# Attention over 7x7 windows: probabilities as the stationary operand, values as 18 moving columns

## The reference

```python
# layer 0: a convolution whose weights are made from the image itself, then a residual
# layer 1: a shifted-window transformer block
h = layer_norm(x); h = roll(h, (-3, -3)); xw = windows_7x7(h).reshape(-1, 49, 48)
q, k, v = split(xw @ w_qkv + b_qkv)             # 6 heads of 8 channels; q scaled
attn = q @ k.T + rel_bias + window_mask         # 49 x 49 for each window and head
attn = softmax(attn)                            # over the keys
o = attn @ v                                    # 49 x 8 for each window and head
x = x + unroll(o @ w_proj + b_proj)
y = layer_norm(x); y = conv3x3(y, 48 -> 192); y = gelu(bn1(y)); y = conv1x1(y, 192 -> 48)
return x + bn2(y)
```

## Time and profile before

| | |
|---|---|
| median of three runs | 4128.19 us |
| span of the profiled execution (the page gives no other time for it) | 4125.0 us |
| layer 0 | 0 to about 494 us |
| attention | about 494 to 2757 us |
| feed-forward | from there to the end |
| TensorE matmul busy, share of the span | 96% |
| weight load, VectorE, ScalarE, GpSimd | 72%, 66%, 59%, 57% |
| DMA | 210.38 MB moved, mean 51 GB/s |

### The profile page before, as it was taken

How to read it: one execution, slowest core, us unless ns; L and a number is a source line. 1 busy time by engine, 2 the same in 40 slices (tenths; PEclk the granted TensorE clock), 3 DMA queues, 4 the chain that set the end, 5 groups by cost and what they waited for, 6 DMA issues and landing times. The chain is left out here.

```text
span 4125.0 us, 76120 instructions
## 1 busy us (share of the span) xinstructions
PE 3958.8 (96%) x23156; PEld 2953.8 (72%) x23156; DVE 2712.5 (66%) x5076; ACT 2451.7 (59%) x4724; POOL 2335.8 (57%) x2216
## 2 busy tenths in 40 slices
PE   7888799999999999999999999969999999999999
PEld 3555577777777777777777777747777777777776
DVE  4454388888888888888888888854444444444443
ACT  3333177777777777777777777744444444444444
POOL 1111266666666666666666666635656565656554
PEclk8888799999999999999999999979999999999999
DMA  4331201111111111111111111125454545454442
GB/s 101 94 94 47 59 20 27 27 26 25 26 27 27 27 27 27 27 26 26 27 27 27 26 25 27 27 52 91 72 95 73 94 74 91 77 87 80 85 83 45
DMA packets 219355, 210.38 MB, mean 51 GB/s; under 512 B 113968, under 2 KB 214320, under 8 KB 216240
## 3 DMA queue, kind: packets, MB, share of 16 engines
q1 hardware_dynamic: 219312, 209.86, 25.1%
HBM read 132.00 MB, written 77.76 MB: 51 GB/s over the span
## 5 line engine op out<-in xcount | busy, mean ns | idle before, releaser
L1222 POOL TENSOR_TENSOR hid_lo<-hid,hid_hi 96x448 fp32r<-96x448 f32 x448 | 770.7, 1725 | 583.2 <-ACT hid_hi L1295 583.1
L590 POOL TENSOR_TENSOR kex<-ks,cw 112x294 f32<-112x294 f32 x1024 | 727.6, 745 | 88.2 <-ACT ks L852 88.2
L1292 ACT ACTIVATE hid<-ps_h,cw 96x448 f32<-96x448 f32 x448 | 323.6, 722 | 728.4 <-PE ps_h L1243 728.4
L683 PEld LDWEIGHTS ps_o<-pt,vex 98*118 98x118 f32 x6144 | 695.1, 183 | 56.4 <-ACT pt L882 2.6
L683 PE MATMUL ps_o<-pt,vex 98*118 98x118 f32 x6144 | 727.0, 268 | 0.5 <-ACT pt L882 0.5
L1354 DVE SCALAR_TENSOR_TENSOR xr<-ps_f,cw,xr 48x448 f32<-48x448 f32 x224 | 151.3, 676 | 773.7 <-PE ps_f L1254 773.7
L656 PE MATMUL ps_s<-kex,qbd 112*98 112x294 f32 x2048 | 592.0, 411 | 0.0
L1239 PE MATMUL ps_h<-ya_hi,wa_hi 128*96 128x448 f32 x1344 | 501.4, 373 | 28.8 <-DVE yb_sp L1328 28.8
L1239 PE MATMUL ps_h<-ya_hi,wa_lo 128*96 128x448 f32 x1344 | 498.6, 371 | 0.0
L1239 PE MATMUL ps_h<-ya_lo,wa_hi 128*96 128x448 f32 x1344 | 498.3, 371 | 0.0
L1015 DVE TENSOR_TENSOR s<-s,mx 98x588 f32<-98x588 f32 x512 | 466.5, 911 | 17.5
(11 more groups left out here) (153 smaller groups left out, 7081.4 us busy)
## 6 DMA issues: line engine op xcount, KB each, us to landing
ya<-y_chunks SPq DMA_DIRECT2D x64, 532.9 KB, 6.9
y_chunks<-y SPq DMA_DIRECT2D x256, 76.1 KB, 1.8
xin<-x_chunks SPq DMA_DIRECT2D x256, 73.5 KB, 2.5
x_chunks<-xo SPq DMA_DIRECT2D x256, 73.5 KB, 1.8
out<-xr SPq DMA_DIRECT2D x32, 588.0 KB, 8.2
yb<-y_chunks SPq DMA_DIRECT2D x96, 177.6 KB, 8.2
xr<-x_chunks SPq DMA_DIRECT2D x32, 514.5 KB, 5.5
xt<-x SPq DMA_DIRECT2D x16, 840.0 KB, 17.2
```

The costliest lines, as they stand in the source:

```text
L590: pool.tensor_tensor(kex[a][:, win, :, :], ks[:, win, :].unsqueeze(1).to_broadcast([PP, HEADS, N]), w("head").unsqueeze(2).to_broadcast([P ...
L683: mm = pe.matmul(ps_o[0:OP, (win % 4) * OP:(win % 4 + 1) * OP], vex[a][:, win, j, 0:OP], pt[d % 2][:, start:start + OP], start=j == 0, sto ...
L1222: pool.tensor_tensor(hid_lo[:, U % slots, :], hid[:, U % slots, :], hid_hi[:, U % slots, :], ALU.subtract).then_inc(hid_lo_set, 1)
L1292: act.activation(hid[:, U % slots, :], ps_h[U % slots][0:half, 0:T1], ACT.Gelu, bias=w("t1")[:, U % 2:U % 2 + 1], scale=w("s1")[:, U % 2:U ...
```

## The change

Transposed probabilities: `pt` gets one buffer for each of the four duos, and holds key rows by (window, head pair, image, query). `values` runs once per half chunk (four windows). For each window, head pair and image there is one matmul: stationary are the 49 columns of `pt` for that image, moving are 18 columns of `vs` (8 channels of the one head, 8 of the other, and two columns of ones, one per head). Image 0 writes PSUM partitions 0 to 48, image 1 writes 64 to 112, so the result has queries on the partitions. VectorE takes the reciprocal of the two sums per query and multiplies (`outputs`), giving `on`. TensorE turns it back to channels on partitions (`outputs` on TensorE: 16 matmuls against the identity `pick`, 49 columns moving, the images again in the two column halves), and ScalarE copies it to `ot` for `project`. `denominators`, the two reciprocal steps on ScalarE and the product on GpSimd are gone.

Further edits: the twelve operations that fill `vex` become two per chunk (product with an ownership mask `own`). The subtraction of the maximum for duo 1 moves from VectorE to GpSimd. The scale and shift of `y` move from VectorE to ScalarE. GpSimd copies the second half of `h` instead of computing it again. The residual is loaded from DRAM by two more DMAs per chunk instead of being made from `xin` on VectorE, and its bias is added within the residual sum. Preparation loses the zeroing of `vex` and 32 small copies.

```diff
 # buffers
-        vex = [sb(f"vex{a}", [2 * N, NWC, HEADS // 2, 2 * BO]) for a in range(2)]
+        vs = [sb(f"vs{a}", [2 * N, NWC * 2 * (HEADS // 2), VW]) for a in range(2)]
-        pt = [sb(f"pt{i}", [2 * N, 2 * HN + OP - 2 * N]) for i in range(2)]
+        pt = [sb(f"pt{d}", [2 * N, 2, HEADS // 2, 2, N]) for d in range(DUOS)]
 # TensorE (QP = 64 + 49, VW = 18)
-            def values(n, d, a):
+            def values(n, half, a):
...
+                for i in range(4):
+                    win = 4 * half + i
                     for j in range(HEADS // 2):
-                        start = i * HN + j * 2 * N
-                        mm = pe.matmul(ps_o[0:OP, (win % 4) * OP:(win % 4 + 1) * OP], vex[a][:, win, j, 0:OP],
-                                       pt[d % 2][:, start:start + OP], start=j == 0, stop=j == HEADS // 2 - 1)
+                        for img in range(2):
+                            block = (win * 2 + img) * (HEADS // 2) + j
+                            mm = pe.matmul(ps_o[BO * img:BO * img + N, (i * (HEADS // 2) + j) * VW:(i * (HEADS // 2) + j + 1) * VW],
+                                           pt[win // 2][:, win % 2, j, img, :], vs[a][:, block, :], start=True, stop=True)
+            def outputs(n, a):
+                pe.wait_ge(o_set, n * 2 + 2)
+                if at_edges(n + 1)[2]:
+                    pe.wait_ge(v_set, n * 2 + 5)
+                for win in range(NWC):
+                    for img in range(2):
+                        mm = pe.matmul(ps_m[1][BO * img:BO * img + C, win * N:(win + 1) * N], on[a][:, win, :],
+                                       w("pick")[:, img * N:(img + 1) * N], start=True, stop=True)
 # TensorE body of chunk n
                 scores(n, 0, a)
-                    values(n - 1, 2, 1 - a)
...
                 scores(n, 1, a)
-                    values(n - 1, 3, 1 - a)
+                    values(n - 1, 1, 1 - a)
...
                 scores(n, 2, a)
                     variance2(n - 2)
-                values(n, 0, a)
                     pe.wait_ge(ln2_done, n - 1)
...
-                    denominators(n - 1, 1 - a)
                 transposes(n, 1)
                 scores(n, 3, a)
-                        pe.wait_ge(lnd_done, n)
                     keys(n + 1)
                     value_rows(n + 1, 0)
-                values(n, 1, a)
+                values(n, 0, a)
+                    outputs(n - 1, 1 - a)
                     value_rows(n + 1, 1)
                 transposes(n, 2)
                     project(n - 1)
 # GpSimd body: split_squares(n+1), split_squares2(n-2), then
-                    normalize2(n - 2, m - 1, a)
-                    twice(n + 1)
-                    divide(n - 1, 1 - a)
+                shift(n)                # tensor_tensor subtract, 98 x 588, duo 1
+                    before_twice(n + 1)
+                    normalize2(n - 2, m - 1, a)
+                    twice()             # tensor_copy(h[:, :, 1, :], h[:, :, 0, :])
                     keys(n + 1, 1 - a)
 # ScalarE: outputs(n - 1, 1), reciprocals(n - 1), outputs(n, 0) gone from the body; new
+                    y_affine(n - 2, a)  # after exps(n, 2)
+                    outputs(n - 1)      # last: ot <- ps_m[1]
 # VectorE
+            def outputs(n, half, a):
+                dve.reciprocal(rden[half][:, :]..., part[:, :, 2 * HD:VW]).then_inc(rden_set, 1)
+                dve.wait_ge(rden_set, n * 2 + half + 1)
+                dve.tensor_tensor(on[a]..., part[:, :, 0:2 * HD]..., rden[half]...to_broadcast(...), ALU.mult).then_inc(o_set, 1)
-                for head in range(HEADS):
-                    ins = dve.tensor_scalar(to[...], rows[:, :, :, own], w("couple")[:, head % 2:head % 2 + 1], None, op0=ALU.mult)
+                dve.tensor_tensor(vs[a][:, half * blocks:(half + 1) * blocks, 0:2 * HD], ps_m[1 - half]..., w("own")..., ALU.mult)
 # SyncE, per chunk: load_ahead(n), load_residual(n), store(n - 2)
+            def load_residual(n, a):
+                if at_edges(n)[0]:
+                    sp.wait_ge(x2_set, n - 1)
+                for i in range(2):
+                    sp.dma_start(xres[a][BO * i:BO * i + C, :, :], x1s[n, C * i:C * i + C, :]...).then_inc(xres_in[a], 16)
```

More of the change, by code:

```diff
@@ L53 @@
 CHUNKS = RC * B // 2
-OP = BO + C + HEADS
+QP = BO + N
+VW = 2 * HD + 2
 HN = HEADS * N
@@ L463, in attention @@
         y_out = [sem(f"y_out{a}") for a in range(2)]
-        wrapped, xres_set = sem("wrapped"), sem("xres_set")
+        xres_in = [sem(f"xres_in{a}") for a in range(2)]
+        wrapped = sem("wrapped")
         center_mm, xc_copied, squared, var_mm, ln_done, rstd_done, h_done, h_twice = (
@@ L536, in _ @@
             load(1, 1)
-            load_ahead(0, 0)
-            load_ahead(1, 1)
+            sp.wait_ge(zeroed, 1)
+            for n in range(2):
+                load_residual(n, n)
+            for n in range(2):
+                load_ahead(n, n)
             with sp.Fori(1, CHUNKS // 2 - 1) as m:
@@ L541, in _ @@
                     load_ahead(m * 2 + a, a)
+                    load_residual(m * 2 + a, a)
                     store(m * 2 + a - 2, a)
-            for n in range(CHUNKS - 4, CHUNKS):
+            for n in range(CHUNKS - 2, CHUNKS):
+                load_residual(n, n % 2)
+                store(n - 2, n % 2)
+            for n in range(CHUNKS - 2, CHUNKS):
                 store(n, n % 2)
@@ L613, in body @@
                     split_squares2(n - 2)
+                shift(n)
+                if after:
+                    before_twice(n + 1)
+                if before2:
                     normalize2(n - 2, m - 1, a)
                 if after:
[L616 to L619 removed]
+                    twice()
                     keys(n + 1, 1 - a)
             split_squares(0)
[L623 removed]
+            before_twice(0)
+            twice()
             keys(0, 0)
@@ L801, in _ @@
             variance2(n - 1)
-            values(n, 3, 1)
-            pe.wait_ge(lnd_done, n)
-            denominators(n, 1)
+            values(n, 1, 1)
             pe.wait_ge(ln2_done, n)
+            outputs(n, 1)
             project(n)
@@ L853, in keys, with outputs @@
                                ACT.Identity, bias=bks[:, :]).then_inc(k_set, 1)
[L855 to L868, removed]
+            def outputs(n):
+                act.wait_ge(ot_mm, n + 1)
                 if at_edges(n)[1]:
-                    act.wait_ge(odiv_set, n)
-                act.activation(rden[:, :], lnd[:, :], ACT.Exp, scale=-1.0).then_inc(rden_set, 1)
+                    act.wait_ge(proj_mm, n)
+                act.activation(ot[:, :, :].rearrange("c r (w k) -> c w r k", w=NWC),
+                               ps_m[1][0:PP, 0:T2].rearrange("c (w r k) -> c w r k", w=NWC, r=WS), ACT.Copy).then_inc(ot_set, 1)
             def exps(n, d):
-                act.wait_ge(shifted, n * DUOS + d + 1)
+                if d == 1:
+                    act.wait_ge(pool_shifted, n + 1)
+                else:
+                    act.wait_ge(shifted, n * (DUOS - 1) + (1, 0, 2, 3)[d])
                 act.activation(s_sb[d % 2][:, :, :], s_sb[d % 2][:, :, :], ACT.Exp).then_inc(exp_done, 1)
@@ L965, in _ @@
             rsqrt2(n)
+            y_affine(n, 1)
         @block.vector
         def _(dve):
-            for a in range(2):
-                ins = dve.memset(vex[a][:, :, :, :], 0.0)
-            ins.then_inc(zeroed, 1)
+            dve.memset(ps_o[BO // 2:BO, :], 1.0).then_inc(o_rows_set, 1)
             dve.wait_ge(weights_in, 16)
@@ L1064, in body @@
                     shift(n, d)
+                if before:
+                    outputs(n - 1, 1, 1 - a)
                 if after:
@@ L1467, in packed_attention @@
         "center": diagonal(np.eye(C) - 1 / C), "sum": diagonal(np.ones((C, C))),
-        "head": both(head), "eps": np.full(PP, EPS, np.float32), "couple": np.kron(np.eye(2), np.ones((N, 1))), "vones": vones, "den": den,
-        "ident": np.eye(2 * N),
+        "head": both(head), "eps": np.full(PP, EPS, np.float32), "couple": np.kron(np.eye(2), np.ones((N, 1))),
+        "own": np.kron(np.eye(2), np.ones((N, HD))), "ident": np.eye(2 * N), "pick": pick,
     })
```

177 lines of the change are left out of this document (80 added, 97 removed).

## The result

The changed kernel takes 3989.06 us (median of 4 runs, 3985.74 to 3994.79) against 4128.01 us (4 runs, 4124.60 to 4130.14): ratio 0.9665, 95% interval 0.9652 to 0.9677. The forecast was 3990. Its profiled span is 3990.3 us, 134.7 less than before.

The account below looks back on a forecast made before the run. TensorE was taken to bound attention, until other engines' chains are longer: a chunk falls from 17.34 to 16.27 us, 1.07 times 127 is 136, plus 2 for the start, span 3987, time 3990 us; range 3850 to 4110.

Parts of the forecast that it names:

- The walk of the prediction: One attention chunk followed from the start of scores(n, 0) through the engines' chains: 16.27 us instead of 17.34.
- Pace of the new passes: Values blocks on TensorE: 42 ns a pass per half, both halves at once; 1.02 us, 1.35 with width changes.
- Rival (c): Values blocks and turn back: halves run one after the other; 18.8 us a chunk, 4315 us; chance 0.07.
- Rival (d): New TensorE passes: spaced by handing out instructions, whatever their size; at 85 ns near 5010 us; chance 0.07.
- Rival (e): TensorE's clock falls to 1.2 GHz as new passes stream little; a tenth of the time there, 4180; chance 0.04.
- Two chains: Before transposes(n, 1): GpSimd's subtraction with exponential, and layer norm with queries, both meet at about 9.5 us.
- GpSimd's subtraction of 588 elements: Duo 1's moved subtraction before its exponential: taken as 1.72 us, between 1.53 and 2.26, ending at 8.57.
- The sign that the prediction gave: TensorE idle before transposes(n, 1), behind GpSimd, would show the forecast right; no size given.
- The other chain: Layer norm from variance(n+1) at 5.17: queries 3.2 to 3.8 us later, transposes(n, 1) at 9.0 to 9.6.
- rival (b): Chains longer than walked (GpSimd, copy of `h`, table additions): 0.8 to 1.2 us a chunk, 4090 to 4140; chance 0.08.
- Rival (a): Waits before queries and transposes(n, 1) close; TensorE's 15.12 us set the chunk, about 3845 us; chance 0.14.
- The start: Preparation before attention: the lost zeroing of `vex` shortens it by about 2 us.

Follow-up runs that it names:

- same_half: Changed kernel with image 1's values matmuls writing image 0's PSUM partitions, so all use one column half (part of the result lost): 4313.17 us, ratio to before 1.0446.
- copy_norm: Changed kernel with GpSimd's copy of h ahead of its normalize (as a product with ones) and the norm steps reordered on ScalarE and TensorE: 3884.67 us, ratio 0.9418.
- sub_dve: Changed kernel with duo 1's subtraction moved back from GpSimd to VectorE: 3992.33 us, ratio 0.9668.
- norm_order: Changed kernel, order only: ScalarE's centered2 before the exponential, ln, rsqrt, ln2 before duo 0's copy; TensorE's variance2 before scores(n, 2): 3951.53 us, ratio 0.9586.
- copy_first: Changed kernel with GpSimd copying h before it normalizes, written as a product with ones: 3940.89 us, ratio 0.9553.
- grouped: Changed kernel with all 12 matmuls of image 0 in a values block before those of image 1, both halves used: 4229.85 us, ratio 1.0255.
- by_three: Changed kernel with the image changing after every three matmuls in values blocks: 4016.82 us, ratio 0.9740.
- twice_values: Changed kernel with every values matmul issued twice: 4270.37 us, ratio 1.0347.

## Why the prediction was right

The time came out at 3989 because what bounds the chunk was named rightly: a shorter TensorE program, and then the wait ahead of queries. That it came out within 1 us of the forecast is luck: two errors of 0.4 us cancelled. The walk of the prediction, from the start of scores(n, 0), against after; the part after transposes(n, 1) is read from 1503.19 on in the timeline above:

| step | predicted us | measured us |
|---|---|---|
| variance(n+1) starts | 5.17 | 5.13 |
| queries start | 8.4 to 9.0 | 8.34 |
| transposes(n, 1) start | 9.50 | 9.07 |
| from there to the values block | 3.01 | 3.40 |
| values block and turn back, to value rows | 1.89 | 1.96 |
| value rows, transposes, projection | 1.87 | 1.96 |
| this chunk | 16.27 | 16.39 |
| mean chunk | 16.27 | 16.30 |

**Pace of the new passes.** Right: 42 ns per pass and half from the earlier trace rows, 46 to 48 measured. A block was put at 1.35 us with its changes of width; after shows 0.10 going in (scores take 1.09 and not 0.99 to the block) and 1.21. Rival (c) names a real effect, but its 4315 beside the 4313 of `same_half` is chance: (c) had the turn back serial as well, which `same_half` leaves in two halves, and it had not the clock, which cost some 45 us. Rival (d), passes spaced by issue at 85 ns, falls with after itself (23 ns) and a fixed spacing of any size falls with `same_half` (48 ns for the same passes). Rival (e) did not come: the granted clock is 1.00 in the chunk shown and does not fall between 600 us and the last chunks. The Trainium skill ("TensorE: Matmul & The Clock Gate", section "Wait — 56ns, not 53.3ns?") has about 25 ns from start to start as a floor; here 48 passes start within 1.12 us, 23 ns apart, over two halves.

**The chain to transposes(n, 1).** Two chains were said to meet at 9.5. One failed in size and in rank. GpSimd's subtraction of 588 elements was put at 1.72 us with a lower bound of 1.53; after shows, in rows from the timelines of four engines:

```profile
1516.13 1.02 POOL L590 TENSOR_TENSOR sq_lo<-sq,sq_hi 112x392 fp32r<-112x392 f32 x1 [0.72 <-ACT sq_hi L897]
1517.10 1.18 POOL L603 TENSOR_TENSOR s<-s,mx 98x588 f32<-98x588 f32 x1
1518.10 0.61 DVE L1035 TENSOR_TENSOR h<-xc,rstd 112x392 f32<-112x392 f32 x1 [1.64 <-ACT rstd L850]
1518.16 0.59 ACT L901 ACTIVATE lnv<-ps_m,cw 112x392 f32<-112x392 f32 x1 [0.19 <-PE ps_m L719]
1518.64 0.68 ACT L881 ACTIVATE s<-s 98x588 f32<-98x588 f32 x1
1518.85 0.90 PE L715 MATMUL ps_m<-h,wqs 112*112 112x392 f32 x2 [0.73 <-ACT lnv L901]
```

It takes 1.18 us and ends at 1518.28, 7.77 after scores(n, 0) and not 8.57 as walked; 0.24 of the difference is the split before it (1.02 us, put at 1.26). The exponential starts at 1518.64 because ln2 stands before it on ScalarE. The sign that the prediction gave, idle time before transposes(n, 1), is absent: they follow queries by 0.73 us. The lower bound was taken from groups with two full operands (745 ns for 294 elements); extrapolating from them failed. The second operand here, one maximum repeated 49 times, is the likely reason: in `copy_norm` the copy of `h` as a product with ones, 392 elements with the second operand repeated 49 times, takes 0.85 us, and the product for `y`, 392 elements with two full operands, 1.02. `sub_dve` confirms that the move is free.

The other chain alone holds the point: variance, ScalarE's logarithm, the copy of duo 0's transposes, ScalarE's second step of the norm (`rstd`), VectorE's product `h`, queries. The profile puts the wait down to L901, the logarithm of the second norm, for which queries wait too; but in 115 chunks each of after and of `norm_order` queries start 0.145 us after the end of `h`, within 0.002. In after L901 ends beside `h` (1518.75 and 1518.71); in `norm_order` it ends at 1510.19, `h` at 1510.42, queries start at 1510.56. `norm_order` takes the copy out of this chain, and there queries start 7.77 us after scores(n, 0), at 1510.56 after 1502.79, 0.57 earlier than in after.

**The step left out.** From transposes(n, 1) to the values block the walk had only TensorE's own work. Value rows wait for the copy of `h` on GpSimd, 1.05 us, behind the product for `y`; 0.37 us in this chunk. The prediction had this copy only in rival (b), at 0.8 to 1.2 us with its fellows. `copy_first` removes the wait (keys start 0.67 us before value rows in all its chunks) and gains 48 us, which shows it.

**Rival (a)**, all waits closed, is what `copy_norm` comes near, at 15.49 us a chunk and 3885 us, not 15.12 and 3845. Its busy share hides what is left: in the stretch above queries start 1.21 us after scores where 0.99 is their own work, 0.14 after VectorE ends `h`, and transposes(n, 1) start 0.82 after queries where 0.67 is, 0.05 after ScalarE ends the exponential. These two waits, the same in every chunk looked at, are 0.37 us. So the sum of TensorE's work, 15.12, was nearly right, and the norm and the exponential still set the pace at this place.

**The start** was to gain 2 us for the zeroing of `vex`. It did not: TensorE's first matmul of attention is at 499.96 us in after (13.23 idle, released by the weights' DMA), 497.74 before. In the kernel before the same matmul waits for the same DMA (13.04 us idle), so the zeroing was not last. VectorE and ScalarE were covered as said: 13.02 and 12.45 us busy a chunk.

## What to carry to other kernels

Small matmuls gain from the two column halves only if they alternate half by half in program order: the same block cost 1.21 us alternating, 1.32 in threes, 2.15 grouped. When a change shortens the engine that sets the time, walk every producer of its next operands, copies included: here an omitted 1.05 us copy was worth 48 us, and with the order of the queues on three engines changed as well it was 104 us in all, with the same work on TensorE. A busy share of 99.7% (498.32 of 500 us) still hid 0.37 us of waits a chunk: read start to start as well. Take the duration of an unshown operation from rows with the same operand form, or leave the lower bound open.

## What was not expected of the hardware

- In `same_half` the granted clock fell to its lower level for 3 to 10 us at a time, 23 times between 600 us and the last chunks, each time within 1.2 us of the end of a values block of one half, though TensorE was busy 95% of the time (0.93 in 1000 to 1100 us). In `grouped`, with 2.15 us blocks that use first one half and then the other, it fell three times in the same part, each time at the end of such a block; the row below is one (columns as above, granted clock 0.50). In after, in `by_three` and in `twice_values`, whose 2.2 us blocks have twice the passes alternating between the halves, it did not fall there. Both kernels with falls keep to one half through long stretches of a block, the three without change halves every few passes; why this matters is open.

```profile
1361.90:1365.30 3.40, 3.40 (x47) 3.30 (x43) 1.47 (x4) 0.53 (x1) 3.40 (x5) 0.50 0.39 90
```

- The reach of one half ahead of the other is a few passes: about three of image 0's turn back start before the end of image 1's values in `grouped`, and groups of three matmuls (six passes) cost only 0.1 us a block.
- GpSimd takes 2.0 to 2.2 ns an element where the second operand is a repeated value (1174 ns for 588 in after, 0.85 us for 392 in `copy_norm`), 2.6 with two full ones (1020 for 392).
